# Attention scores from exact 12-bit halves in float32r, two heads in row tiles, in place of bf16 thirds in four column tiles

## The reference, cut to what matters

```python
scores = jnp.einsum('bhqk,bhsk->bhqs', q, k) * scale          # attention A
scores = jnp.where(causal, scores, -jnp.inf)
attn_out = jnp.einsum('bhqs,bhsk->bhqk', jax.nn.softmax(scores), v)

att = jnp.einsum('bhqd,bhkd->bhqk', k[:, :, 1:], k)           # attention B: queries are the next keys
mask = t[None, :] <= t[:T - 1, None]
y1 = jnp.einsum('bhqk,bhkd->bhqd', jax.nn.softmax(jnp.where(mask, att, -jnp.inf)), v)
```

## Time and profile before

| what | value |
|---|---|
| median of 3 runs | 3419.71 us |
| lowest, highest run | 3412.88, 3427.87 us |
| span of the profiled execution | 3426.7 us |
| TensorE busy | 2995.8 us, 87% |
| ScalarE busy | 2226.8 us, 65% |
| VectorE busy | 1443.0 us, 42% |
| GpSimd busy | 831.3 us, 24% |
| mean granted TensorE clock | 0.930 |

### The profile page before, as it was taken

How to read it: one execution, slowest core, us unless ns; L and a number is a source line. 1 busy time by engine, 2 the same in 40 slices (tenths; PEclk the granted TensorE clock), 3 DMA queues, 4 the chain that set the end, 5 groups by cost and what they waited for, 6 DMA issues and landing times.

```text
span 3426.7 us, 99594 instructions
## 1 busy us (share of the span) xinstructions
PE 2995.8 (87%) x42980; PEld 1325.4 (39%) x42980; DVE 1443.0 (42%) x3534; ACT 2226.8 (65%) x2487; POOL 831.3 (24%) x1278
## 2 busy tenths in 40 slices
PE   7799988988998699986998888998898887998887
PEld 3333333333433244443443444343333333433343
DVE  5322235455454552334333323445445545422344
ACT  2578866676776377673776666776666664777552
POOL 4111122332322122221222121323233221311111
PEclk9899999999999799997999999999999998999988
DMA  5222212221221123222221222221222211222111
GB/s 139 80 74 72 78 42 69 67 71 57 73 62 49 50 59 95 61 63 63 83 72 57 76 74 81 61 60 50 68 67 70 72 54 33 67 64 77 43 41 49
DMA packets 229870, 226.13 MB, mean 66 GB/s; under 512 B 33221, under 2 KB 212933, under 8 KB 229320
## 3 DMA queue, kind: packets, MB, share of 16 engines
q1 hardware_dynamic: 228504, 217.47, 22.2%
q10 hardware_dynamic: 816, 0.79, 0.1%
HBM read 146.80 MB, written 71.32 MB: 64 GB/s over the span
## 4 chain that ended last, share of the span: by engine, by line
PE 72%; DVE 13%; issue 9%; ACT 3%; SPq 1%; DMA 1%; POOL 0%; DVEq 0%; ACTq 0%; POOLq 0%
PE ps L856 45%; PE ps L1063 24%; ACT probs L812 3%; PE ps L868 3%; DVE pmax L1357 2%; DVE ln_st L1129 2%; DVE xn L1138 2%; DVE nw_u L1119 1%; DVE nw_u L1121 1%; DVE nw_y L1123 1%; DVE x_buf L1250 1%; DVE ln_mv L1132 1%; DVE o_blk L1399 1%; PE ps L966 0%; DVE nw_y L1114 0%
## 5 line engine op out<-in xcount | busy, mean ns | idle before, releaser
L812 ACT ACTIVATE probs<-ps 128x1024 f32<-128x1024 f32 x2176 | 2077.9, 1093 | 823.9 <-PE ps L856 820.5
L856 PE MATMUL ps<-q_st,k_st 99*32 99x384 bf16 (+3 forms) x20480 | 1287.4, 356 | 110.4 <-issue 93.3
L1063 PE MATMUL ps<-probs,v_st 128*17 128x512 f32 (+3 forms) x10240 | 1222.5, 550 | 100.8 <-issue 74.6
L856 PEld LDWEIGHTS ps<-q_st,k_st 99*32 99x32 bf16 x20480 | 568.4, 97 | 925.5 <-issue 534.8
L715 POOL TENSOR_SCALAR_AFFINE_SELECT probs<-probs 128x256 f32<-128x256 f32 (+1 forms) x896 | 406.0, 468 | 1648.0 <-ACT probs L812 1640.3
L1063 PEld LDWEIGHTS ps<-probs,v_st 128*17 128x17 f32 x10240 | 295.1, 100 | 389.5 <-issue 181.1
L1399 DVE STREAM_TRANSPOSE o_blk<-ps 128x512 f32<-128x512 f32 x128 | 90.7, 709 | 449.9 <-PE ps L1063 448.0
L856 PE MATMUL ps<-xT,wT 128*32 128x512 f32 x2048 | 253.8, 615 | 1.8 <-issue 1.8
L1250 DVE TENSOR_TENSOR x_buf<-x_buf,ps 128x512 f32<-128x512 f32 x64 | 43.7, 683 | 397.8 <-PE ps L856 397.8
L868 PE MATMUL ps<-ident,xn 128*128 128x128 f32 x512 | 97.5, 323 | 117.1 <-DVE o_blk L1399 58.5
L639 POOL TENSOR_TENSOR parts<-rest,parts 128x512 bf16<-128x512 f32 x96 | 119.1, 1240 | 227.6 <-DVE parts L1161 227.6
(11 more groups left out here) (136 smaller groups left out, 2174.3 us busy)
## 6 DMA issues: line engine op xcount, KB each, us to landing
part_a<-parts SPq DMA_DIRECT2D x192, 128.0 KB
x_buf<-in_L_attn_a_X SPq DMA_DIRECT2D x32, 512.0 KB, 4.6
q_st<-part_a SPq DMA_DIRECT2D x128, 128.0 KB
o_chan<-o_out SPq DMA_DIRECT2D x64, 256.0 KB, 2.3
o_in<-o_chan SPq DMA_DIRECT2D x64, 256.0 KB, 4.4
q_st<-part_b SPq DMA_DIRECT2D x128, 128.0 KB
k_st<-part_a SPq DMA_DIRECT2D x64, 192.0 KB, 2.9
part_b<-parts SPq DMA_DIRECT2D x96, 128.0 KB
```

The source lines that it names most:

```text
L812: nc.scalar.activation(probs[:, g % NP_BUF, :], ps[:, bk:bk + 2, :].rearrange("p a n -> p (a n)"), ACT.Exp, scale=SCALE[ATT[g // (NHG * NG ...
L856: last = pe.matmul(o[c:c + 32], kt[:, c:c + 32], q, **how)
L1063: last = pe.matmul(ps[32 * j:32 * j + VW, bank, q0:q0 + w], v_st[:, k % 2, kb, hg * HG + j, :], p, start=(kb == 0), stop=(kb >= TB * qc), ...
```

## The change

Keys and queries are split into two fp32 numbers: the high half keeps the upper 20 bits (a mask with -4096, which leaves 12 bits of mantissa with the implied one), the low half is the exact rest. Four products of halves, 64 rows, make a score. `k_st` and `q_st` are fp32, with even heads in rows 0 to 63 and odd heads in rows 64 to 127, and read by TensorE as float32r. A score product is one instruction with all 128 keys as weights; the two heads of a slot, one for each PSUM bank, are issued next to each other. The maxima move out of the contraction to `m_st`, a bf16 tile of 12 rows at partition 32 (three for each head), and are added in flagged instances by a product of their own with the selecting weights `m_sel`. VectorE makes the high half (and in P the low one), GpSimd the low half of B's keys and the squares of P, ScalarE makes none. DMAs store two halves of 256 KB instead of three parts of 128 KB, and load 4 pieces of keys and 6 of queries per chunk instead of 3 and 5; the rows of zeros are not loaded with each chunk any more.

```diff
-K_PART = (0, 1, 2, 0, 1, 0)
-Q_PART = (0, 0, 0, 1, 1, 2)
-K_RUNS = ((0, 0, 3), (3, 0, 2), (5, 0, 1))
-Q_RUNS = ((0, 0, 1), (1, 0, 1), (2, 0, 2), (4, 1, 2))
-MROW = DK * len(K_PART)
-KROWS = MROW + 3
+HALVES = 2
+KROWS = 4 * DK
+K_RUNS = ((0, 0, 2), (2, 0, 2))
+Q_RUNS = ((0, 0, 2), (2, 1, 1), (3, 0, 1))
+HIGH_BITS = -4096
+MROW = 32
...
-        k_st = sb("k_st", [P, HG, S], BF16)
-        q_st = sb("q_st", [P, HG, S], BF16)
+        k_st = sb("k_st", [P, HG // 2, S])
+        q_st = sb("q_st", [P, HG // 2, S])
+        m_st = sb("m_st", [MROW + 3 * HG, S], BF16)
...
+        def keys(j):
+            return k_st[KROWS * (j % 2):KROWS * (j % 2 + 1), j // 2, :].bitcast(F32R)
+
+        def queries(j):
+            return q_st[KROWS * (j % 2):KROWS * (j % 2 + 1), j // 2, :].bitcast(F32R)
...
 def place_maxima(n):
-                    for c in range(NCH):
-                        sp.wait_ge(s_q[c], 16 * (len(Q_RUNS) + 1) * (n + 1))
+                    if n:
+                        sp.wait_ge(s_scores, n * NG)
...
-                                sp.dma_start(q_st[MROW + r:MROW + r + 1, j, :].rearrange("o (t q) -> o t q", t=NT),
-                                             m_part[r][:, :]).then_inc(s_mx["placed"], 16)
+                                sp.dma_start(m_st[MROW + 3 * j + r:MROW + 3 * j + r + 1, :].rearrange("o (t q) -> o t q", t=NT),
+                                             m_part[r]).then_inc(s_mx["placed"], 16)
                         with sp.Else():
-                            sp.sem_inc(s_mx["placed"], 48)
+                            sp.dma_start(m_st[MROW + 3 * j:MROW + 3 * j + 3, :], rows_d).then_inc(s_mx["placed"], 16)
+                            sp.sem_inc(s_mx["placed"], 32)
...
 def scores(g, masked):
-                for bank, units in enumerate(GROUPS[i]):
-                    o = ps[:, 2 * (g % NS_BUF) + bank, :]
-                    for qc, kb, j, q0, w, col in units:
-                        mask = masked and kb >= TB * qc
-                        last = matmul(o[:, col:col + w], k_st[0:KROWS, j, kb * P:(kb + 1) * P],
-                                      q_st[0:KROWS, j, qc * CH + q0:qc * CH + q0 + w], start=True, stop=not mask,
-                                      skip_group_check=mask)
-                        if mask:
-                            last = matmul(o[:, col:col + P], mask_qk[:, :], ident_b[:, :], start=False, stop=True,
-                                          skip_group_check=True)
+                for pair in zip(*GROUPS[i]):
+                    for bank, (qc, kb, j, q0, w, col) in enumerate(pair):
+                        o = ps[:, 2 * (g % NS_BUF) + bank, :]
+                        at = qc * CH + q0
+                        last = pe.matmul(o[:, col:col + w], keys(j)[:, kb * P:(kb + 1) * P], queries(j)[:, at:at + w],
+                                         start=True, stop=not masked, skip_group_check=masked)
+                        if masked:
+                            mask = kb >= TB * qc
+                            last = pe.matmul(o[:, col:col + w], m_sel[:, j, :], m_st[MROW:MROW + 3 * HG, at:at + w], start=False,
+                                             stop=not mask, skip_group_check=True)
+                            if mask:
+                                last = pe.matmul(o[:, col:col + P], mask_qk[:, :], ident_b[:, :], start=False, stop=True,
+                                                 skip_group_check=True)
...
+            def high_half(u, src):
+                return nc.vector.tensor_scalar(parts[:, u % NPARTS, 0, :].bitcast(I32), src.bitcast(I32), HIGH_BITS, None,
+                                               ALU.bitwise_and)
```

More of the change, by code:

```diff
@@ L8 @@
 I32 = mybir.dt.int32
+F32R = mybir.dt.float32r
 ACT = mybir.ActivationFunctionType
@@ L69, in head_group @@
         g = len(groups)
[L70 removed]
+        groups.append([[(qc, d + 2, n, 2 * P, 2 * P, 0), (qc, d + 2, n + 2, 2 * P, 2 * P, 2 * P)]
                        for n in range(2)])
[L72 removed]
+        sets.append((g, qc, d + 2, [(g, j % 2, j, 2 * P, 2 * P, 2 * P * (j // 2)) for j in range(HG)], 1))
     return groups, sets
@@ L218 @@
 number(("P", "MA"), "unit", lambda j: 4 if j.kind == "P" else 2)
-UNIT_STORES = [3 + 3 * (j.kind == "MA" and j.c == 0) for j in JOBS if j.kind != "MB"
+UNIT_STORES = [2 + 2 * (j.kind == "MA" and j.c == 0) for j in JOBS if j.kind != "MB"
                for _ in range(4 if j.kind == "P" else 2)]
+SQUARED = {j.at["unit"] + i: 4 * j.at["p"] + i + 1 for j in JOBS if j.kind == "P" for i in range(4)}
 NPARTS = 4
@@ L495, in load_keys @@
                 src = part_a[b % 2, 1] if a == "A" else part_b[b % 2]
[L496 to L499, removed]
+                for par in range(2):
+                    for r, part, rows in K_RUNS:
+                        at = KROWS * par + r * DK
+                        sp.dma_start(k_st[at:at + rows * DK, :, c * CH:(c + 1) * CH],
+                                     src[part * DK:(part + rows) * DK, hg * HG + par:(hg + 1) * HG:2,
+                                         c * CH:(c + 1) * CH]).then_inc(s_k[c], 16)
             def load_queries(n, c):
@@ L508, in load_queries @@
                 src = part_a[b % 2, 0] if a == "A" else part_b[b % 2]
[L509 to L515, removed]
+                first = c * CH + (a == "B")
+                for par in range(2):
+                    for r, part, rows in Q_RUNS:
+                        at = KROWS * par + r * DK
+                        sp.dma_start(q_st[at:at + rows * DK, :, c * CH:(c + 1) * CH],
+                                     src[part * DK:(part + rows) * DK, hg * HG + par:(hg + 1) * HG:2,
+                                         first:first + CH]).then_inc(s_q[c], 16)
             def place_maxima(n):
@@ L649, in p_job @@
                     yield j.t0 + T_P[f"u{i}"] + 2
-                    low_part(j.at["unit"] + i)
+                    if i == 0:
+                        ffn = [o for o in JOBS if o.t0 < j.t0 and o.kind != "P"]
+                        if ffn:
+                            pool.wait_ge(s_part, ffn[-1].at["r1"].n + 1)
+                        if j.at["p"]:
+                            pool.wait_ge(s_part, [o for o in JOBS if o.t0 < j.t0 and o.kind == "P"][-1].at["n1"].n + 1)
+                    pool.wait_ge(*emptied(j.at[f"u{i}"]))
+                    high = parts[:, (j.at["unit"] + i) % NPARTS, 0, :]
+                    pool.tensor_tensor(squares[:, i, :], high, high, ALU.mult).then_inc(s_sq, 1)
             def m_job(j):
@@ L755, in p_job @@
                         nc.scalar.copy(xT[:, j.at["chan"] % 2, kt, :], ps[:, part.bank, :]).then_inc(s_side[part.bank], 1)
-                for i in range(4):
-                    yield j.t0 + T_P[f"u{i}"]
-                    u, part = j.at["unit"] + i, j.at[f"u{i}"]
-                    act.wait_ge(s_part, part.n + 1)
-                    if u >= NPARTS:
-                        act.wait_ge(s_store[u % NPARTS], stored(u - NPARTS))
-                    nc.scalar.copy(parts[:, u % NPARTS, 0, :], ps[:, part.bank, :]).then_inc(s_high, 1)
                 for i in range(2):
```

113 lines of the change are left out of this document (54 added, 59 removed).

## The result

The changed kernel takes 4121.8 us (median of 4 runs, 4102.2 to 4123.0) against 3418.5 before: ratio 1.205, 95% interval 1.201 to 1.209. The direction was forecast, the size was not: 3530 was said, and 4122 lies far over the range that ended at 3780.

The account below looks back on a forecast made before the run. TensorE was taken to set the time, except in stretches of plain slots. Unflagged -140, flagged +245 and masks +5 made +110 us; on the median 3419.7 that gave 3530, own range 3440 to 3620, 8-in-10 range 3340 to 3780.

Parts of the forecast that it names:

- costed at zero: Work moved among VectorE, ScalarE and GpSimd, and extra DMA loads and bytes: off TensorE's chain, zero for all.
- The flagged instances: Four of 32 instances: second full-width product, no pairing, two shape changes a unit; 61 us each after waits, +245 us.
- the unflagged ones: 28 instances without a flag: paired scores less shape changes save 5.4 us in 20, 4 in 8; 140 us saved.
- the maxima stretches: Maxima phase before flagged instances: stays VectorE's; 16 masks a flagged head with two changes, +5 us in all.
- a turn was costed at 0.2 us: TensorE's change of array shape between scores and other work: 0.10 us in, 0.095 out, 39 round trips an instance, 7.6 us.
- The rate of float32r and the pairing: Score products: one cycle a column, two row tiles together, saving 14.75 us an instance; failure of either a 16% rival.
- 7.2 forecast for an unflagged instance: Net saving on scores without a flag: 14.75 us from pairing less 7.6 us of shape changes.
- capped this only in the first four instances and near the end: Eight light instances: ScalarE's 0.91 us a slot and three score buffers limit TensorE's lead; 4 us saved each.
- less 17 for VectorE: 17 of 68 slots precede waits for VectorE's norm chain, where time won is waited again; leaves 5.4 us of 7.2.
- 4% as a rival: Clock falls to 1.2 GHz in flagged instances, doubling 59 us of scores and maxima: +236 us, 3766; chance 4%.
- My rival of 123 us: Second head's weight load exposed after each change of shape: 4.4 us in 28 instances, 123 more, 3650; chance 10%.
- The all-free rival: Flagged products overlap and all changes of shape are free: 290 us saved in unflagged instances, about 3230; chance 4%.

Follow-up runs that it names:

- experiment 3: Changed kernel with odd heads reading the rows of even ones, so the two score products of a slot cannot run side by side: 4548.6 us.
- experiment 2: Changed kernel with keys and queries read as bf16, the upper 16 bits of each fp32 word at every second element: 3909.6 us.
- experiment 4: Changed kernel, flagged instances reordered: both scores of a pair, then both 12-row maxima products, then both masks: 3707.6 us, ratio 1.084 to the kernel before.
- experiment 5: As experiment 4, but maxima products padded with zeros to 64 rows, in the row tile of their head: 3542.8 us, ratio 1.035 to the kernel before.
- experiments 1: Kernel before, with each bf16 score product and diagonal mask issued as one 128-column instruction instead of four column tiles: 3596.6 us, ratio 1.053.
- experiment 6: Products of experiment 5 in the changed kernel's order: score, maxima product and mask of one head, then of the other: 3650.5 us.

## Why the prediction was wrong

**What bounds the kernel.** Right: TensorE set the time before and does after; ScalarE waited more, not less. VectorE, ScalarE and GpSimd, costed at zero, are busy for less time, and the data queue uses 21.5% of its engines against 22.2% in the earlier trace rows, with a fifth more bytes over a longer span.

**Where the forecast of +110 us and the 693 of the spans part.** The flagged instances cost 648 instead of 245, the unflagged ones, without the maxima stretches, 16 instead of -140, the maxima stretches 19 instead of 5, start and end 9 instead of nothing. Two steps failed above all: the granted clock was left out of the flagged sum (some 320 us, by the estimate below), and a turn was costed at 0.2 us where it takes 0.36 (0.16 x 39 x 28 = 175 us, and some 80 more in the flagged instances). The rest of this section takes them one by one.

**The rate of float32r and the pairing.** Both assumptions held. I took one cycle a column, 0.217 us; it is 0.23 to 0.24 (experiment 3). The bf16 pairs of experiment 2 take the same 0.24, so the difference is not float32r's. The two row tiles run together without loss.

**The turn.** This term was mis-sized. I had 0.10 in and 0.095 out from the earlier trace rows, 0.2 us a round trip. Out it is 0.09; in it is 0.12, and the first float32r pair pays 0.10 more (experiments 2 and 3). With 0.02 for each of two pairs that is 0.35 us; the timeline's 0.79 less 0.434 of streaming gives 0.36, 0.16 more than taken. I had even a row for it: the load of fp32 weights repeats every 0.112 us, and I called it hidden but for narrow pieces. If the inference of experiment 2 holds, that is the error: behind a turn there is nothing to hide it. Times 39 turns it is 6.2 us of the 7.2 forecast for an unflagged instance.

**What is left.** 1.0 us net should still have been won, and 0.4 were lost. Experiment 2 says more: without the 0.10, 3.9 us should have come back and 1.9 did. TensorE's weight loads for scores waited 705 us in 920 places for ScalarE in the changed kernel, against 191 us in 598 places in the earlier trace rows; this row of the waits is from the changed kernel:

```profile
PEld ps L1038 <- ACT probs L829: 704.9, 920, 1.7
```

In plain slots ScalarE's 0.91 us a slot is the pace, and time won on TensorE there becomes waiting; and where such a wait parts the two pairs of a batch, the second pays the 0.10 again (starts 0.42 apart instead of 0.34). The prediction capped this only in the first four instances and near the end. By its own arithmetic ScalarE needs 67 of 98 us, but those 67 lie in stretches of their own: about 42 of the 68 slots of an unflagged instance with a full job ran at ScalarE's pace in the changed kernel (exponentials at most 0.96 us apart), 43 before, so mainly the other 26 could give anything. That step failed as well: I counted the whole 68 slots as TensorE's, less 17 for VectorE. How the remaining 1.4 us (1.0 + 0.4) divide between ScalarE's pace, repeated loads, waits for VectorE and the granted clock (0.942 over the 24 instances, 0.948 before) was not separated; no run isolates ScalarE's pace.

**The flagged instances.** The sum had every part but one, and a wrong size in one. Second product, no pairing, two changes a unit: right, and experiments 4 and 5 undo them one after the other. At full clock a unit costs 0.75 us where I had 0.62, 0.10 of it what experiment 2 takes away with the dtype: 0.13 x 160 = 20 us more. The part left out of the sum is the clock. I gave it 4% as a rival. Its price there, 59 us an instance, was right in kind and too low: a unit takes 1.26 us at 1.2 GHz instead of 0.75, so the 195 us at that level would be some 116 at full clock. These 79 us (an estimate) are half of the excess of 158, and with the 61 forecast and the 20 above they make it up. The argument against it, that dense value work lies between, was wrong: value products take 53 of the first instance's 257 us, value and side work together a third, and the clock fell all the same.

**The maxima stretch.** I held it for VectorE's. That was so before; in the changed kernel TensorE is busy for 22.8 of 23.2 us there, at 1.2 GHz, where three products of 512 columns take 1.57 us, 0.52 each. My figure for the masks was also too low by my own terms: 16 masks in each of four flagged heads with two changes of 0.095 are 12 us, not 5. Measured are 18 from the first to the last score product, 19 from exponential to exponential.

**The start.** I put the stores and loads at zero. The chain of work in the first 130 us goes through SyncE, which waits for stored halves to land before it issues the next loads; two such waits stand there in the changed kernel, then one of the kernel before:

```profile
58.09 8.16 DMA part_a<-parts
79.27 6.57 DMA part_a<-parts
```

```profile
76.57 3.73 DMA part_a<-parts
```

The next block of x lands at 103.8 instead of 97.2 us, and the first exponential starts 8.2 later. All kernels of the new layout have this start (6 to 9 us); which of the larger stores and the two more loads a chunk makes it was not tested.

The Trainium skill's rule that a change of tiling mode drains the engine (TensorEngine Tiling, Key Properties) agrees with experiments 1 and 5. Its rule that weight loads of differing row groups overlap (TensorE: Matmul & The Clock Gate, Part 3) agrees too, as far as a pair shows it: its two products, and the records of their loads, start 3 to 4 ns apart even behind a turn. My rival of 123 us for a second exposed load is out; what I missed is the 0.10 that the first pair pays. The all-free rival was misadded, too: 290 saved and 100 paid make 3230 only if flagged instances still pay for changes that it calls free.

**What stays open.** The lower level of the clock went with alternating shapes at each product (changed kernel: 0.62), was mostly gone with half as many changes (0.84) and gone with the pairs in one shape (0.98). Whether it is the turns themselves, products that stand alone or the gaps between streams was not told apart; from the changed kernel to 4 and 5 all three fell together, and in 6 most products pair after all. The maxima stretch, at 0.50 with turns only at its 16 masks, speaks against the turns as the only cause. No version tried beats the kernel before; the best of the new layout, experiment 5, is 3.5% slower.

## What to carry to other kernels

A change that makes a product cheaper on an engine that alternates between array shapes has to be costed per batch between two turns: here 0.12 us in, 0.09 out and 0.10 for the first pair with fp32 weights eat seven tenths (0.31 of 0.44 us) of what pairing saves in a batch of two pairs, and of the rest nothing reached the end. Where a small correction product must follow each large one, give it the same tile shape by padding its rows with zeros, and issue pairs together: the two were worth 579 us here, 471 of it by the shape alone (experiment 6). And before counting a saving for all slots, count the slots that run at another engine's pace.

## What the runs showed of the hardware that was not expected

- Float32r products of 64 rows and 128 columns stream 512 columns in 0.23 us, and two in different row tiles in 0.24 (experiment 3, changed kernel); bf16 pairs read at every second element take the same 0.24 (experiment 2).
- Row tiles run their products independently: with a maxima product of the first head issued between them, the scores of two heads still start 6 ns apart (experiment 6). With a maxima product of another shape in that place they never did in the flagged instances (changed kernel).
- The first fp32-weighted product after a change of shape, or after a wait of the array, holds 0.10 us longer than its successors (0.34 against 0.24); in bf16 it does not (experiment 2).
- Products that alternate between 64 and 32 rows for most of a stretch ran at 1.2 GHz for 195 of 257 us with TensorE never idle in the records; the same products ordered in pairs brought the mean granted clock from 0.62 to 0.84 (experiment 4).
